# Slot order of VectorE, the first weight tiles and the first slot's row numbers in a decoder block with experts

## The reference

```python
x = x + rg_lru(layernorm(x))                       # two projections, a gated scan over 100 steps, a projection
x = x + cross_attention(ctx_1024, layernorm(x))    # 8 heads, 722 media keys and the 100 latents themselves
x = x + ffn(layernorm(x))                          # the part that the change is about

# ffn: 800 tokens of 512 numbers, 8 experts, each token goes to one
route = sigmoid(x @ Wr + br)
max_prob, max_ind = max(route, 1), argmax(route, 1)
for e in range(8):
    y = gelu(x @ W1[e]) @ W2[e]                    # W1[e]: 512 x 2048, W2[e]: 2048 x 512
    out = out + (max_ind == e) * y
out = out * max_prob
```

## Time and profile before

| | us |
|---|---|
| median of 3 runs | 1048.96 |
| lowest and highest | 1046.52, 1049.16 |
| the profiled execution | 1049.56 |
| its span, first to last instruction | 1047.8 |
| PE busy in the span | 1026.5 |
| VectorE busy in the span | 811.1 |
| ScalarE busy in the span | 560.6 |

### The profile page before, as it was taken

One profiled execution on the slowest core, in us unless ns is written; L12 is line 12 of the kernel. 1 busy time (PEld: TensorE's weight loads), 2 busy tenths in 40 slices (PEclk: granted clock), 3 DMA queues, 4 the chain that ended last, 5 costly groups with the idle time before them and its releaser, 6 DMA issues.

```text
span 1047.8 us, 18264 instructions
## 1 busy us (share of the span) xinstructions
PE 1026.5 (98%) x6115; PEld 938.2 (90%) x6116; DVE 811.1 (77%) x1401; ACT 560.6 (53%) x1108; POOL 112.4 (11%) x95
## 2 busy tenths in 40 slices
PE   8999999999999999999999999999999999999997
PEld 7979998999999999999999999998977887788886
DVE  7888666888979889798897987675668956847992
ACT  3525565545545455454554445672455846837871
POOL 2622200000000000000000000000111210211221
PEclk9999999999999999999999999999999999999999
DMA  8433984344323433234332343488258955946970
GB/s 274 125 119 129 313 293 168 84 166 125 107 94 94 169 124 108 93 95 169 123 109 93 95 139 131 149 286 310 91 174 284 353 214 183 344 165 227 359 265 22
DMA packets 108533, 182.45 MB, mean 174 GB/s; under 512 B 31742, under 2 KB 50686, under 8 KB 106576
## 3 DMA queue, kind: packets, MB, share of 16 engines
q1 hardware_dynamic: 106816, 177.45, 50.2%
q0 software_dynamic: 1680, 4.53, 1.2%
HBM read 145.84 MB, written 37.10 MB: 175 GB/s over the span
## 4 chain that ended last, share of the span: by engine, by line
PE 77%; DVE 8%; DMA 5%; issue 4%; ACT 3%; SPq 1%; DVEq 0%; ACTq 0%; POOL 0%; POOLq 0%
PE bank L636 22%; PE bank L638 22%; PE bank L637 22%; PE bank L1156 4%; DMA stage<-in_W 2%; PE bank L1297 1%; PE bank L1143 1%; PE bank L1174 1%; DMA w<-in_WoT 1%; PE bank L1141 1%; PE bank L1173 1%; DVE wsl L1616 1%; ACT wsh L1472 1%; SPq L675 1%; DVE hs L1685 1%
## 5 line engine op out<-in xcount | busy, mean ns | idle before, releaser
L636 PE MATMUL bank<-pt_h,xn_h 128*128 128x256 f32 (+1 forms) x576 | 167.2, 290 | 0.0
L638 PE MATMUL bank<-pt_h,xn_l 128*128 128x256 f32 (+1 forms) x576 | 164.8, 286 | 0.0
L637 PE MATMUL bank<-pt_l,xn_h 128*128 128x256 f32 (+1 forms) x576 | 164.7, 286 | 0.0
L1616 DVE TENSOR_TENSOR wsl<-stage,wsh 128x2048 fp32r<-128x2048 f32 x63 | 143.3, 2289 | 22.2 <-ACT wsh L1472 20.0
L636 PE MATMUL bank<-xt_h,qt_h 128*128 128x410 f32 (+1 forms) x384 | 136.4, 355 | 0.8 <-ACT pr L1427 0.8
L637 PE MATMUL bank<-xt_l,qt_h 128*128 128x410 f32 (+1 forms) x384 | 134.1, 349 | 0.0
L638 PE MATMUL bank<-xt_h,qt_l 128*128 128x410 f32 (+1 forms) x384 | 134.1, 349 | 0.0
L1472 ACT CAST wsh<-stage 128x2048 fp32r<-128x2048 f32 x63 | 120.6, 1917 | 17.3 <-PE bank L638 11.2
L636 PEld LDWEIGHTS bank<-pt_h,xn_h 128*128 128x128 f32 x576 | 109.0, 189 | 0.8
L637 PEld LDWEIGHTS bank<-pt_l,xn_h 128*128 128x128 f32 x576 | 109.1, 189 | 0.0
L638 PEld LDWEIGHTS bank<-pt_h,xn_l 128*128 128x128 f32 x576 | 109.0, 189 | 0.0
(11 more groups left out here) (262 smaller groups left out, 2425.3 us busy)
## 6 DMA issues: line engine op xcount, KB each, us to landing
stage<-in_W SPq DMA_DIRECT2D x63, 1024.0 KB, 6.9
scr_q<-st SPq DMA_DIRECT2D x16, 800.0 KB, 4.3
qf<-scr_q SPq DMA_DIRECT2D x8, 1600.0 KB, 6.6
zr<-scr_z SPq DMA_DIRECT2D x16, 800.0 KB, 5.6
scr_z<-zf SPq DMA_DIRECT2D x7, 1600.0 KB, 5.2
rt<-in_ctxT SPq DMA_DIRECT2D x7, 1444.0 KB, 12.9
raw<-in_ctx SPq DMA_DIRECT2D x8, 768.0 KB, 4.5
mrow<-scr_rows SPq DMA_DIRECT2D x14, 361.0 KB, 3.9
```

Of the source, the lines that this page charges most:

```text
L636: pe.matmul(dest, lh, rh, start=start and k == 0, stop=False)
L637: pe.matmul(dest, lh, rl, start=False, stop=False)
L638: last = pe.matmul(dest, ll, rh, start=False, stop=stop and k == n - 1)
L1616: return dve.tensor_tensor(dst, src, high.bitcast(F32), ALU.subtract)
```

## The change

It has three parts. (1) Behind the scan VectorE computes the ranks of expert 0's tokens alone (`rank0`: the token's rank plus one if it is expert 0's, else 0) and compares them with 1 to 128 (`iota` grows by a column for this). PE multiplies the result with the token numbers (`tokr`), and VectorE makes `idx0`, the row numbers of slot 0, from which the first gather starts. Then low part 4 is made, then the old chain runs as before (its waits count one or two further). (2) The tail's list takes the weight tiles 0 to 3 instead of 0 to 2, the first two right behind the value products; Y6 is cut in 5 and 3 heads with L4 and T5 between; the loads of tiles 4 to 6 are issued one token tile sooner. (3) VectorE gets a list of its own for a slot, `dve_plan`, while PE and ScalarE keep `slot_plan`. The numbers of filler products change.

```diff
@@ tail @@
-            ("Y", 3), ("A", 3), ("B", 3), ("H", 0), ("Y", 4), ("A", 4), ("B", 4), ("T", 3), ("H", 1),
-            ("Y", 5), ("A", 5), ("L", 3), ("B", 5), ("T", 4), ("H", 2), ("Y", 6), ("A", 6), ("B", 6), ("L", 4),
-            ("T", 5), ("T", 6), ("L", 5), ("L", 6)]
+            ("H", 0), ("H", 1), ("Y", 3), ("A", 3), ("B", 3), ("H", 2), ("Y", 4), ("A", 4), ("B", 4), ("T", 3), ("H", 3),
+            ("Y", 5), ("A", 5), ("L", 3), ("B", 5), ("T", 4), ("Y", 6), ("L", 4), ("T", 5), ("y", 6), ("A", 6), ("B", 6),
+            ("L", 5), ("T", 6), ("L", 6)]
@@ a slot, VectorE @@
+    dve_plan = [("W", 0), ("H", 1), ("W", 1), ("W", 2), ("G", 1), ("H", 2), ("W", 3), ("X", 1), ("H", 3), ("W", 4), ("W", 5),
+                ("R", 0), ("K", 1), ("W", 6), ("W", 7), ("H+", 0)]
+                    elif what == "H+":
+                        if not (last and e is last_expert):
+                            split_hidden(n + 1, k)
@@ SyncE @@
-                if b >= 4:
-                    load_weights(0, 0, range(b, b + 1))
+                if b < NT - 1:
+                    load_weights(0, 0, range(b + 1, b + 2))
@@ GpSimd @@
-            gather(idx[:, 0:1])
+            gather(idx0[:])
+            pool.wait_ge(s_idx, 2)
@@ PE, behind L1254 @@
-            keep_running(bank[3], wsh[0][:, 0, :], 18)
+            keep_running(bank[3], wsh[0][:, 0, :], 5)
+            for b in range(NT):
+                if b % HALF == 0:
+                    pe.wait_ge(s_ohi, b // HALF + 1)
+                r = tile_rows(b)
+                last = pe.matmul(bank[5][:, 0:2], ohp[0:r, b, :], tokr[0:r, b, :], start=b == 0, stop=b == NT - 1)
+            last.then_inc(s_tp, 1)
+            keep_running(bank[3], wsh[0][:, 0, :], 24)
...
-            keep_running(bank[3], wsh[0][:, 0, :], 16)
+            keep_running(bank[3], wsh[0][:, 0, :], 3)
@@ ScalarE @@
-            high_weights(0, 3)
+            act.wait_ge(s_yd, NT)
+            high_weights(0, 4)
             act.wait_ge(s_lm, 1)
             act.activation(vals[:, :, 2], lmx[:], ACT.Sigmoid).then_inc(s_gate, 1)
-            act.wait_ge(s_yd, NT)
-            for q in range(4, NW):
+            for q in range(5, NW):
@@ VectorE, behind the scan @@
+            ch.add(dve.tensor_tensor(rank0[:], bank[0][:, 0:NT * E].rearrange("p (b e) -> p b e", e=E)[:, :, 0], upto[:, 0, 0:NT],
+                                     ALU.add))
+            ch.join()
+            ch.add(dve.scalar_tensor_tensor(rank0[:], rank0[:], 1.0, oh[:, 0:NT, 0].bitcast(F32), ALU.add, ALU.mult))
+            ch.join()
+            for part in range(2):
+                bs = slice(part * HALF, min((part + 1) * HALF, NT))
+                n = [P, bs.stop - bs.start, P]
+                ch.add(dve.tensor_tensor(ohp[:, bs, :], iota[:, 1:P + 1].unsqueeze(1).broadcast_to(n),
+                                         rank0[:, bs].unsqueeze(2).broadcast_to(n), ALU.is_equal))
+                tally(s_ohi)
...
+            dve.wait_ge(s_tp, 1)
+            ch.add(dve.tensor_scalar(idx0[:], bank[5][:, 0:1], float(NTOK), None, ALU.add))
+            tally(s_idx)
+            low_weights(0, 4)
...
-            low_weights(0, 3)
...
-            low_weights(0, 4)
             norm_tokens(0)
             keep_tokens(0)
             split_tokens(0)
             low_weights(0, 5)
             low_weights(0, 6)
             low_weights(0, 7)
+            split_hidden(0, 0)
```

More of the change, by code:

```diff
@@ L234, in build @@
     tokv = mem("tokv", [P, NT])
-    iota = mem("iota", [P, P])
+    iota = mem("iota", [P, P + 1])
     before = mem("before", [P, P])
@@ L385, in build @@
     idx = mem("idx", [P, NSLOT], I32)
+    idx0 = mem("idx0", [P, 1], I32)
+    tokr = mem("tokr", [P, NT, 2], F32R)
+    rank0 = mem("rank0", [P, NT])
     sm = mem("sm", [P, NSLOT, 3])
@@ L1194, in finish @@
                             ).then_inc(s_vp, 1)
-                    elif what == "Y":
+                    elif what in "Yy":
                         half, r = int(b >= T_A), tile_rows(b)
@@ L1203, in finish @@
                             pe.wait_ge(s_x2, b - 1)
-                        for h in range(HEADS):
+                        heads = range(HEADS)
+                        if b == NT - 1:
+                            heads = heads[5:] if what == "y" else heads[:5]
+                        for h in heads:
                             pe.wait_ge(s_otl, ot_done(half * HEADS + h))
@@ L1208, in finish @@
                                                   h == 0, h == HEADS - 1)
-                        last.then_inc(s_yd, 1)
+                        if HEADS - 1 in heads:
+                            last.then_inc(s_yd, 1)
                     elif what == "C":
@@ L1260, in _ @@
                     pe.wait_ge(s_ohi, b // HALF + 1)
+                r = tile_rows(b)
[4 more added lines that the diff above has]
+                if b % HALF == 0:
+                    pe.wait_ge(s_ohi, b // HALF + 3)
                 r = tile_rows(b)
@@ L1888, in finish @@
                             ch.add(dve.memset(oh[:, NT, :].bitcast(F32), 0.0))
+                            ch.add(dve.tensor_copy(tokr[:], tokv[:].unsqueeze(2).broadcast_to([P, NT, 2])))
                     elif what == "C":
@@ L2004, in positions @@
                 bs = slice(part * HALF, min((part + 1) * HALF, NT))
-                ch.add(dve.tensor_tensor(ohp[t, bs, :], iota[t].unsqueeze(1).broadcast_to([P, bs.stop - bs.start, P]),
+                ch.add(dve.tensor_tensor(ohp[t, bs, :], iota[t, 0:P].unsqueeze(1).broadcast_to([P, bs.stop - bs.start, P]),
                                          pin[t, bs].unsqueeze(2).broadcast_to([P, bs.stop - bs.start, P]), ALU.is_equal))
@@ L2026, in _ @@
             tally(s_ohv)
-            dve.wait_ge(s_tp, 1)
+            dve.wait_ge(s_tp, 2)
             ch.add(dve.tensor_scalar(idx[:], bank[2][:, 0:NSLOT], float(NTOK), None, ALU.add))
@@ L2031, in _ @@
             tally(s_ctl)
-            low_weights(0, 3)
-            dve.wait_ge(s_tp, 2)
+            dve.wait_ge(s_tp, 3)
             ch.add(dve.tensor_copy(sm[:].rearrange("p s v -> p v s"),
@@ L2056, in split_tokens, with split_hidden @@
                 low(xg_l[:], bank[4][:].rearrange("p (c t) -> p c t", c=ND), xg_h[:]).then_inc(s_xtl, 1)
+            def split_hidden(n, k):
+                dve.wait_ge(s_hth, n * NF + k + 1)
+                low(ht_l[k % 2][:], bank[2 + k % 2][:].rearrange("p (c t) -> p c t", c=4), ht_h[k % 2][:]
+                    ).then_inc(s_htl, 1)
             def slot(n, e, last):
-                for what, k in slot_plan:
+                for what, k in dve_plan:
                     if what == "G":
@@ L2071, in slot @@
                     elif what == "H":
-                        dve.wait_ge(s_hth, n * NF + k + 1)
-                        low(ht_l[k % 2][:], bank[2 + k % 2][:].rearrange("p (c t) -> p c t", c=4), ht_h[k % 2][:]
-                            ).then_inc(s_htl, 1)
+                        split_hidden(n, k)
+                    elif what == "H+":
+                        if not (last and e is last_expert):
+                            split_hidden(n + 1, k)
                     elif what == "R":
@@ L2122 @@
         "ones": np.ones((P, P), np.float32),
-        "iota": np.broadcast_to(np.arange(P, dtype=np.float32), (P, P)).copy(),
+        "iota": np.broadcast_to(np.arange(P + 1, dtype=np.float32), (P, P + 1)).copy(),
     }
```

## The result

| | before | after |
|---|---|---|
| median, us | 1047.87 (4 runs) | 1062.53 (4 runs) |
| lowest and highest | 1046.52, 1049.16 | 1061.63, 1066.51 |
| the profiled execution | 1049.56 | 1066.51 |
| its span | 1047.8 | 1064.8 |

The changed kernel is slower: ratio 1.0147, 95% interval 1.0117 to 1.0178, and the medians are 14.7 us apart (a ratio is estimated from all the runs and can differ from that of the medians by 0.1%). 1050.6 was forecast, at most 1055.5. The profiled execution is the slowest of its four, 17.0 us over that of before. Where they lie is found with three marks that both traces have: the last low part of the attention's output (V15), the first expert product, and the first turning of each slot.

The account below looks back on a forecast made before the run. PE, busy 98% of the span, was taken as the bound. Start of the stage +1.1 and slots +0.5 (4.2 new waits against 3.6 + 0.1 won) gave +1.6 us: 1050.6 forecast, range 1045.5 to 1055.5.

Parts of the forecast that it names:

- The tail: End of the tail, before routing: low parts and Y6's split delay the last logits about +0.5 us, taken as +0.1.
- The own chain: Slot 0's routing: old chain 4.5 us later, gather earlier, normalizing +1.0; with the tail, first expert product +1.1 us.
- rival 3: PE's clock halved at another place, at the first expert products: up to 1.7 us more, 1052.3; chance 0.08.
- VectorE's queue at H+: At a slot's end the queue stands until the semaphore; first weight low part 3.45 or 4.35 us behind first turning (P).
- Rival 1: Between slots the queue runs ahead of H+'s semaphore, slots win 4.1: 3.0 us faster, 1046.0; chance 0.20.
- The new waits of slots 3 and 6: In the expert's second slots PE waits for the last turned values' low part, 0.76 us each.
- The eighth load: Each slot's eighth weight load, issued behind W3, takes 5.0 us and lands 19.8 us behind the first turning.
- 0.56 + 3 x 0.71: New PE waits from the late load: 0.56 us in slot 1, 0.71 each in slots 4, 7 and 8.
- rival 2: Expert-stage loads become the bound, lateness handed on through ScalarE and VectorE: at 6.5 us a load +7.6, 1056.6; chance 0.22.

Follow-up runs that it names:

- g1: Kernel before with the changed tail alone (part 2), old routing chain and old slot list: 1052.90 us against 1049.73, ratio 1.0028.
- e4: Whole change with weight loads halved from the second expert on (values wrong): 1049.13 us against 1049.31 of the kernel before, ratio 0.9990.
- k2: Kernel before; normalizing, third and fourth turned values, tokens' split one tile sooner in VectorE's list, weight tile 6 behind the slot's result: 1047.51 us against 1049.91.
- k1: Kernel before; normalizing, turned values' low parts, tokens' split one tile sooner, first turned values' low part at the previous slot's end: 1057.36 us against 1049.91.
- e3: Whole change with the first turned values' low part at the head of VectorE's slot list instead of the previous slot's end: 1054.36 us against 1049.31 before.
- e2: Changed kernel with VectorE back on the common slot list, so parts 1 and 2 alone: 1053.53 us against 1049.31 of the kernel before.
- f1: Kernel before with only the normalizing of the next tokens one weight tile sooner in VectorE's list: 1046.87 us against 1049.73, ratio 0.9973.
- g3: e2 with the fifth weight tile's low part moved out of the routing chain, behind the row numbers: 1051.93 us against 1049.73 of the kernel before.
- h1: e2 with 12 instead of 24 filler products ahead of the row numbers' product: 1053.76 us against 1049.28 of the kernel before.
- c2: g3 with 12 filler products and f1's list together: 1046.26 us against 1049.28 of the kernel before, ratio 0.9973.

## Why the prediction was wrong, step by step

**The tail: +0.5 for the last logits, +0.1 net.** Right in the changed kernel: VectorE's maximum of the logits (L1980) comes 28.22 us behind the mark instead of 27.67, the scan no later at all. What I priced at nothing, the low part that is gone from the gather's shadow and with it the next load that now falls into the gather, costs nothing only because the gather starts early; g1 has the same tail without the early gather and loses 3.2.

**The own chain.** Right: the old chain starts 4.4 us later (4.5 said), the gather 2.65 earlier (2.4), and the normalizing is held by the table of means, not by the gather. It starts 1.63 later, not 1.0, and the first expert product 2.2, not 1.1. The difference between 1.1 and 2.2 is of the size of rival 3: 0.9 us in the fourteen products and 0.6 from normalizing to product, all at half clock. e4, the same code up to there, ran this stretch at full clock (1.00 from 770 to 802), and there it is +0.8. So +1.1 was the right size without the clock, and rival 3 had too small a chance: of the seven kernels with both parts all but e4 ran 5.8 to 13 us at half clock between mark and first product, those with the old routing 2.4 to 3.4 (k2 6.8).

**VectorE's queue at H+.** Right, in moment and size: first weight low part at P + 3.48 in slot 0 (3.45 said) and P + 4.32 in slot 3 (4.35 said). The rule of the Trainium skill ("Perfetto Trace Analysis", DVE / Act Engine Instruction), by which the queue would have run ahead, is not borne out here: 1.48 us idle behind H+ here, 1.36 in k1, none in e3. The rule speaks of an instruction that already lies in the wait queue; the kernel asks for this wait by a call of its own (`dve.wait_ge`), and no view shows on which instruction it is carried, so why the queue stands is open. Rival 1 falls.

**The new waits of slots 3 and 6, 0.76 each.** Right where nothing else is late: e4 has 25.12 and 25.09 against its 24.25.

**The eighth load: "I take 5.0".** This is the step that failed. In the trace of after the eighth loads took 5.4 us in slot 0 (issued 818.9), 7.4 in slot 1 (844.7) and 6.8 to 7.0 in the other five weight slots, although each was issued 3.8 to 3.9 us behind the one before it. The 5.0 was taken from a load issued at 814.6, which in the kernel before is not the eighth but the one behind it. The eighth loads themselves took 6.4 to 8.1 us there in all seven slots; in slot 0:

```profile
L828 SPq DMA_DIRECT2D stage<-in_W x1: 373/373/373, 810.7 to 810.7; - x1
...
DMA to landing us min/median/max: 6.5/6.5/6.5
```

The sum took 0.56 + 3 x 0.71 for the late load in four slots, as waits for low parts at a slot's end, and none for the GELU values at its start; measured, slots 1, 4, 7 and 8 take 27.64, 27.40, 27.55 and 25.60, together 10.6 over four clean ones of 24.40 where the sum had 2.7, and the lateness reaches slots 3 and 6 too (26.57 and 26.37). I had written the loop down as rival 2 (at 6.5 us a load +7.6, chance 0.22) and cut it off by the 5.0. With four buffers a load is issued when a low part is done, and when VectorE is late all of them are late; in before the DMA engines are already full in such a slot (share 1.00, window below), so there was no room to catch up.

**What the sum lacked: VectorE's own budget.** The windows of slot 1 in before and after, same columns as above:

```profile
823.90:848.40 24.50, 24.50 (x118) 19.99 (x117) 22.87 (x18) 19.59 (x18) 5.51 (x4) 1.00 1.00 352
```

```profile
828.40:856.07 27.67, 24.94 (x117) 19.75 (x115) 24.39 (x19) 20.57 (x19) 7.76 (x5) 1.00 0.96 321
```

VectorE works 22.87 us of a slot of 24.40 in before and has 1.5 to spare. With the first weight low part at P + 3.45, the rest of the list (22.87 less H+'s 0.6) ends at P + 25.7, and the next H+ is due at P' + 1.36 = P + 25.76. Nothing is left: any wait of VectorE within the slot goes on to the next one. My step followed the list only to H3. e4 shows the fit (24.25), the change what one late load does to it.

**The first two parts** lose 4.2 us in the timed runs (e2), where 1.1 was said. In e2's profiled execution (+4.6 in the span) the first expert product comes 2.4 later behind the mark. 0.8 of it are the chain, as in e4; the other 1.6 go with some 10 us at half clock, in which the 24 fillers took 7.45 us instead of 5.74. Another 1.6 lies in the slots, at a granted clock of 1.00, where two slots of the old list came out longer (the first 26.21 and the eighth 26.51), and 0.6 ahead of the mark. So the halved clock is at most a part, and what the rest is stays open: e2's slowest run has its lowest mean clock and its fastest the highest (1055.12 at 0.988, 1050.70 at 0.998), but no run here forced the clock, and f1 shows no such order. g3 and h1 show only that fillers and low part are not it by themselves.

## What to carry to other kernels

Before moving an instruction with a late semaphore to the end of an iteration, add up the engine's whole iteration: its busy time, plus all that its queue must still do behind that semaphore (here 1.5 to 2.3 us of loop code). If nothing is left of the period, every wait inside is handed on, and a stream of loads whose buffers that engine frees becomes later each time. Take the landing time of a load from that same load in every iteration (6.4 to 8.1 us here), not from another one that happens to have the right distance (5.3). And try a reorder one entry at a time: one entry of this list was worth 2.9 us, another cost 7 to 10.

## What the runs showed of the hardware

A 1 MB load took 4.9 to 9.4 us in the expert stage of after, 6.8 in the median, and 6.7 in f1, where ScalarE waits for them only 8.7 us in all: the new order did not slow the loads, it issued them late. At half the size the median is 3.8 and the DMA share of slot 1 is 0.59 instead of 1.00 in before and 0.96 in after. An indirect gather of 256 KB took 5.3 us in before and 7.54 in g1, with one 1 MB load beside it, and 3.4 to 3.6 in g3 and c2, where neither a load nor a weight low part of VectorE ran beside it. The part that GpSimd spends on it was 1.24 us in those two, 2.45 in after and e2, where a weight low part (2.29 us) covers the first 1.3 us of it, 2.77 in g1 (covering 1.7) and 3.12 in before, where two of them run. So low part 4 right behind `idx0`, as part 1 of the change has it, goes with a longer gather, the very one that was to start early: g3, which moves it away in e2, has 3.4 us for 7.2, though there the next load comes later too. In after this cost nothing, since the normalizing waits for the table of means. The reason for GpSimd's longer part is not shown. PE's granted clock fell to 0.50 at another place in nearly every variant of the tail, and once, with the same code, not at all.
